# First split of x in the setup, a wait moved to its first use, and the gate weights' split moved from a batch's first slot to its third

## What is computed

```python
x = L0_conv(x)                      # 128x128 matrix over the channels, from a Ricker filter
t = to_tokens(x)                    # 16 batches, 1024 tokens, 128 channels
t = t + attn(ln(t))                 # linear attention, 8 heads of 16, elu+1 features, causal sums
t = t + ffn(ln(t))                  # per batch: weights W + sum_e g[b,e] * tv_W[e], g from the tokens' mean gate
x = from_tokens(t)

# in ffn
gh = relu(x @ gfc1_w.T + gfc1_b)
g  = (gh @ gfc2_w.T + gfc2_b).mean(over tokens)
W1m = W1 + einsum('be,efd->bfd', g, tv_W1)      # W2m likewise
```

## Time and profile before

| | |
|---|---|
| Median of three runs | 802.8 us (801.71 to 803.27) |
| Profiled execution | 801.26 us, span 799.0 us |
| Setup block | to about 15.9 us |
| Attention block | about 15.9 to 526 us |
| FFN block | from about 526 us |
| Busy over the span | PE 728.1, DVE 676.8, ACT 658.5, POOL 537.4 us |
| `scores_lo` (L805), costliest group on DVE | 175.8 us, 256 times 687 ns |

### The profile page before, as it was taken

The page is one execution under the profiler, slowest core; times in us unless marked ns, Lnnn a source line. Parts: engine busy times, 40 slices in busy tenths (PEclk is TensorE's granted clock), DMA queues, the critical chain, the costliest instruction groups (busy, mean ns, idle before and its releaser), DMA issues. The chain is left out here.

```text
span 799.0 us, 38795 instructions
## 1 busy us (share of the span) xinstructions
PE 728.1 (91%) x11936; PEld 538.6 (67%) x11936; DVE 676.8 (85%) x2605; ACT 658.5 (82%) x1864; POOL 537.4 (67%) x1167
## 2 busy tenths in 40 slices
PE   3869999999999999999999999768999996999993
PEld 2446667667667667667677677556777776677773
DVE  4668899999999999999999999636989875788984
ACT  3658899999999999999999999736888865788884
POOL 2768889999999999999999999610333331133332
PEclk9989999999999999999999999869999999999998
DMA  3475676556566566566565564410122221022222
GB/s 99 91 133 107 136 125 140 125 129 140 129 128 140 128 130 137 128 132 134 128 136 130 131 138 99 91 44 1 41 82 82 80 88 54 1 82 81 81 78 76
DMA packets 202346, 82.63 MB, mean 103 GB/s; under 512 B 176076, under 2 KB 189551, under 8 KB 202232
## 3 DMA queue, kind: packets, MB, share of 16 engines
q1 hardware_dynamic: 202296, 81.99, 45.3%
HBM read 22.69 MB, written 17.30 MB: 50 GB/s over the span
## 5 line engine op out<-in xcount | busy, mean ns | idle before, releaser
L805 DVE SCALAR_TENSOR_TENSOR scores_lo<-p_a,scores_hi 128x512 f16<-128x512 f32 x256 | 175.8, 687 | 5.6 <-ACT scores_hi L701 2.4
L701 ACT ACTIVATE scores_hi<-p_a 128x512 f16<-128x512 f32 x256 | 157.8, 620 | 23.7 <-PE p_a L570 18.9
L1312 POOL TENSOR_TENSOR ffn_rstd_shift<-ffn_rstd_shift,consts 128x4 f32<-128x4 f32 x32 | 36.8, 1149 | 130.8 <-DVE ffn_rstd_shift L1271 130.8
L876 POOL CAST qk_parts<-qk_f 128x256 f16<-128x256 f32 x256 | 101.9, 400 | 6.3 <-issue 4.2
L886 POOL TENSOR_TENSOR qk_parts<-qk_f,qk_parts 128x128 f16<-128x128 f32 x256 | 104.6, 431 | 0.9
L1095 PE MATMUL psb<-merged_W_of_batch,h_hi 128*128 128x128 f16 x512 | 94.2, 220 | 4.2 <-DVE h_lo L1249 3.1
L1249 DVE TENSOR_TENSOR h_lo<-h_f,h_hi 128x512 f16<-128x512 f32 x128 | 95.6, 786 | 1.2 <-ACT h_hi L1152 1.2
L1141 ACT ACTIVATE h_f<-psb,merged_b_of_batch 128x512 f32<-128x512 f32 x128 | 87.2, 711 | 11.3 <-PE psb L1076 11.2
L1097 PE MATMUL psb<-merged_W_of_batch,h_lo 128*128 128x128 f16 x512 | 93.8, 219 | 0.0
L1096 PE MATMUL psb<-merged_W_of_batch,h_hi 128*128 128x128 f16 x512 | 93.8, 219 | 0.0
L587 PE MATMUL p_o<-v_parts,scores_hi 128*128 128x17 f16 x1024 | 90.1, 171 | 1.8 <-issue 0.3
(11 more groups left out here) (192 smaller groups left out, 2883.5 us busy)
## 6 DMA issues: line engine op xcount, KB each, us to landing
x_f<-in_x SPq DMA_DIRECT2D x32, 256.0 KB, 3.2
t_rows<-t SPq DMA_DIRECT2D x64, 128.0 KB, 2.0
t_back<-t_rows SPq DMA_DIRECT2D x32, 256.0 KB, 2.7
out<-out_tile SPq DMA_DIRECT2D x32, 256.0 KB, 2.0
tv_share<-in_L_ffn_tv_W SPq DMA_DIRECT2D x32, 128.0 KB
qkT_parts<-qk_parts SPq DMA_TRANSPOSE x128, 3.1
zT_hi_lo<-z_parts SPq DMA_TRANSPOSE x128, 2.3
base_ffn_weights<-in_L_ffn_W SPq DMA_DIRECT2D x2, 256.0 KB, 4.5
```

The source lines that it names most:

```text
L701: nc.scalar.activation(ah[:, t % 2, cols], p_a[:, cols], ACT.Relu).then_inc(ahi_ready[eo], 1)
L805: nc.vector.scalar_tensor_tensor(al[:, t % 2, cols], p_a[:, cols], 0.0, ah[:, t % 2, cols], ALU.max, ALU.subtract).then_inc(alo_ready[eo], 1)
L876: nc.gpsimd.tensor_copy(dst, src.unsqueeze(2).broadcast_to([P, NH, 2, DH])).then_inc(done, 1)
```

## The change

Three edits. The split of the first two tiles of x (`x_hi` on ACT, `x_lo` on POOL) moves from the attention block's first slot to the end of what ACT and POOL do in the setup block; the two buffers are allocated earlier for it. PE's wait for `state_cleared` moves from the block's start to the first `state`. `tv_hi` and `tv_lo` run in s2 instead of s0 of each batch, at the same places in the orders.

```diff
+        xh_ready, xl_ready = sem("xh_ready"), sem("xl_ready")
...
+            xh = sb(early, "x_hi", [P, 2, HALF * P], F16)
+            xl = sb(early, "x_lo", [P, 2, HALF * P], F16)
...
                     for pair in range(TILES // 2):
                         nc.gpsimd.memset(yt[:, 2 * pair, 0:1], 0.0).then_inc(t1_stored[pair], 16)
+                    pool.wait_ge(xh_ready, 1)
+                    nc.gpsimd.tensor_tensor(xl[:, 0, 0:2 * P], xf[:, 0, 0:2 * P], xh[:, 0, 0:2 * P], ALU.subtract)\
+                        .then_inc(xl_ready, 1)
...
                     nc.scalar.activation(bwh[:, :, :], bw[:, :, :], ACT.Copy, scale=WS).then_inc(s_bhi, 1)
+                    act.wait_ge(x_loaded[0], 16)
+                    nc.scalar.activation(xh[:, 0, 0:2 * P], xf[:, 0, 0:2 * P], ACT.Copy).then_inc(xh_ready, 1)
...
                         if n == 0 if isinstance(n, int) else False:
                             pe.wait_ge(ones_set, 1)
+                            pe.wait_ge(state_cleared, 1)
...
                     pe.wait_ge(ones_set, 1)
-                    pe.wait_ge(state_cleared, 1)
...
                     def split_x(b, t):            # on ACT, and the same on POOL
-                        if t % 2:
+                        if t % 2 or isinstance(b, int) and TILES * b + t == 0:
                             return
...
                     def tv_hi(b, t):              # and the same in tv_lo on DVE
-                        if t:
+                        if t != 2:
                             return
```

More of the change, by code:

```diff
@@ L343, in build @@
         with early, ExitStack() as pa_:
-            xh = sb(pa_, "x_hi", [P, 2, HALF * P], F16)
-            xl = sb(pa_, "x_lo", [P, 2, HALF * P], F16)
             eq = sb(pa_, "exp_qk", [P, 4, 2 * C])
@@ L369, in build @@
             sbank = p_s[:, 0:NP * 2 * VW].rearrange("p (a w) -> p a w", w=2 * VW)
-            (xh_ready, xl_ready, conv_done, in_done, bn1, mv1, ve1, rstd1, vhi_ready, exp_ready, relu_ready, vlo_ready,
+            (conv_done, in_done, bn1, mv1, ve1, rstd1, vhi_ready, exp_ready, relu_ready, vlo_ready,
              qk_ready, qhi_ready, khi_ready, lo_ready, su_done, state_cleared, sh_ready, sp_ready,
@@ L375, in build @@
                 sem(s) for s in (
-                    "xh_ready xl_ready conv_done in_done bn1 mv1 ve1 rstd1 vhi_ready exp_ready relu_ready vlo_ready "
+                    "conv_done in_done bn1 mv1 ve1 rstd1 vhi_ready exp_ready relu_ready vlo_ready "
                     "qk_ready qhi_ready khi_ready lo_ready su_done state_cleared sh_ready sp_ready "
```

## The result

Median 796.7 us (794.4 to 800.0, 12 runs) against 802.0 us (799.5 to 804.9, 12 runs): a ratio of 0.9931, 95% interval 0.9913 to 0.9949, or 5.3 us less (the interval is 4.1 to 7.0). The forecast was 5.7 less. The profiled executions differ by 5.0 (spans 799.0 and 794.0).

The account below looks back on a forecast made before the run. The prediction took a ring of POOL's even slot, then PE and DVE in the odd slot, as the bound. Fill -2.25 and loop -3.5 gave -5.75: 797.1 us against 802.8, forecast 794.5 to 799.5, wider range 791.5 to 801.3.

Parts of the forecast that it names:

- Fill, -2.25: Attention stage's start: first statistics 3.15 us earlier, less 0.56 for held POOL and 0.35 in the setup; net -2.25 us.
- the hold on POOL's casts: Batch 0, third slot: `tv_lo` holds POOL's `q_hi` from 20.18 to 20.74, costing the fill 0.56 us.
- the new place in batch 1: Batch 1's moved split, at 49, lies in ACT's pause of 6.73 us until 56.47; nothing gained or lost.
- rival D: Pause after batch 0 ends by something that doesn't move, so the fill's gain is lost: 799.3 us; chance 0.10.
- Collision in the setup: Setup: POOL's `x_lo` and DVE's subtraction at 12.44 exclude each other; cost 0 to 0.67 us, +0.35 taken.
- Loop, -0.25 a batch: Batches 2 to 15: first slot gains 0.75, third slot costs 0.50; net -0.25 a batch, -3.5 us for fourteen.
- rivals A: Third slot takes the split nearly free, state work missing there: cost 0.15, about 792.1 us; chance 0.15.
- B: Third slot costs what the first did, only the fill's -2.25 remains: about 800.5 us; chance 0.19.
- C: Third slot: POOL's hold and DVE's delay follow each other, cost 1.20 a batch: about 806.9 us; chance 0.06.
- The ring: Attention loop: POOL's even slot, then PE and DVE in the odd one, is the bound; DVE and ACT alone have room.
- The sum: Whole kernel: -2.25 of fill and -3.5 of loop make -5.75 us, 797.1 against the median of 802.8.
- The FFN half is only shifted.: FFN block after attention: only starts earlier, with no gain or loss of its own.

Follow-up runs that it names:

- e1: The changed kernel with the share's split back in the first slot, leaving the first split and the moved wait; ratio 0.9996, 801.4 us.
- e2: The kernel before, with only the share's split moved to the third slot; ratio 0.9931, 796.4 us.
- e3: The changed kernel with the share's split in the third slot in batch 0 alone, the first slot in later batches; ratio 0.9956, 799.0 us.
- e5: The changed kernel with the share's split in the second slot of every batch; ratio 0.9937.
- e6: The changed kernel with the share's split in the fifth slot of every batch; ratio 0.9961.
- e10: The changed kernel plus unread PE matmuls behind the last seven gates and while PE waits for the first merge's gates; ratio 0.9926, 796.1 us.
- e4: The changed kernel with POOL's `x_lo` in the setup waiting for DVE's `base_ffn_lo`; ratio 0.9928, 795.4 us.
- e7: The changed kernel with both parts of the share split for only 2 of 256 columns in batches 2 to 15; executed once, 797.2 us.
- e8: The changed kernel with the share's high part made for only 2 of 256 columns in batches 2 to 15; executed once, 799.9 us.
- e9: The changed kernel with the share's low part made for only 2 of 256 columns in batches 2 to 15; executed once, 797.0 us.

## Why the prediction held, and where it did not

- **Fill, -2.25.** Measured -2.25 at the first state. The chain named was right: transfer, `tv_hi`, `tv_lo`, `stats1`. With the share back in s0 (e1) all of the gain is gone; with only the share moved (e2) the fill gains 1.56. The setup lost 0.50 for the 0.35 assumed, of which 0.34 is the copy's and 0.16 was there before POOL's `x_lo` began; the hold on POOL's casts cost 0.47 for 0.56. One reading was off without harm: the new place in batch 1, put at 49, does not lie in ACT's pause, which began at 56.47 - 6.73 = 49.74. It came at 46.49, the pause ran from 47.67 to 53.95, and the lead of 2.52 at its end sinks rival D.
- **Collision in the setup.** In the changed kernel's profile it came with another instruction than I named: not the subtraction at 12.44 with two inputs in SBUF, but the copy with a factor in front of it, 0.57 for 0.23, because the base weights and so ACT came half a microsecond earlier than in the profiled run before. The named collision came as well, in both of the orders that the prediction left open: POOL first in e3, e5 and e6 (1.57 to 1.68 for 1.22; the setup's last DVE instruction 0.36 to 0.49 later than before), DVE first in e10 (`x_lo` 1.71, the end 0.01 later). So what this edit costs in the setup is 0 to 0.5 us by chance of when the base weights arrive (ACT's cast of them starts at 10.47 to 11.06), and the 0.35 was a fair middle. The Trainium skill (SBUF — State Buffer, Who interferes with whom) counts casts and copies with a factor among what can take the shared pair; the 0.57 and e4's 0.53 agree.
- **Loop, -0.25 a batch.** Measured -0.33. Taking it out of s0 gave 0.88 in that pair (0.75 taken, up to 0.83 allowed), putting it into s2 cost 0.54 (0.50 taken). That the delays in s2 lie beside each other and don't add was right, and e7, e8 and e9 show it best: either one alone costs nearly what both do. The pair of 7.78 sinks rivals A (7.3) and B and C (8.0 and more), and e3 shows that the loop's slots are part of the gain.
- **Why s2 is cheaper than s0** is shown only in part. The fifth slot, with state work on all engines, costs 0.66, so missing state work is part of it. But ACT's 0.52 did not vanish in the room that it leaves, as I expected of e9.
- **The ring.** I took POOL's even slot and the other engines' odd slot for one closed ring; then the second slot should have cost 0.5 to 0.8. It cost 0.35. In e5 the pair of s0 and s1 grows, and part of it comes back in the next pair. How is only argued: what comes late in s1 meets s2, where PE has no state work. The ring is a fair account of the even slots and no full model of the loop.
- **The sum.** The term mis-sized is the loop: 14 x 0.33 = 4.6 instead of 3.5. With the fill's 2.25 the parts make 6.9, and 5.3 was measured, with 7.0 as the interval's end. So the nearness of 796.7 to 797.1 is in part luck: the parts gave more than forecast, and some 1.6 us of it doesn't show in the median. Where it stays is open. Batches 2 and 3 and the FFN block each differ by some 4 us from trace to trace, whatever the edit, and the twelve times of the changed kernel spread over 5.6 us.
- **"The FFN half is only shifted."** In the pair of profiled executions it was not: 2.5 of 7.5 us were lost at the two merges, where the half-clock stretches fell on different work. Against e4, the changed kernel with one more wait, the same comparison gives a lead of 6.36 at the last gate and 6.0 at the end. Over all traces the block's time follows no edit of this case. So the sentence is neither shown nor refuted within that scatter, and the prediction had no allowance for it.

## What to carry to other kernels

Ask of a stage's first slot what it waits for that could be asked for earlier or used later; here a piece of side work, placed early in each engine's order, held up the whole fill by its transfer. When a piece of work is moved in a balanced loop, price both places by carrying the rows on, and look for delays that lie beside each other: several engines' parts can cost little more than one of them. And compare the lead at the end of each stage, not only the spans: it can shrink in a stage that no line of the change touches. Before calling that a cost of the change, look at the same stage in every other trace; here it took 270.9 to 275.0 us with the same code.

## What the hardware showed unasked

- POOL and DVE stopped each other in both directions. On POOL `rsqrt2` took 1.00 for 0.55, a cast 0.87 for 0.40, `z_lo` 0.93 for 0.43 and `x_lo` 1.71 for 0.67 (e10); on DVE a copy with a factor took 0.57 or 0.73 (e1) for 0.23, a cast 0.53 for 0.43 and the base weights' subtraction 1.65 for 1.22 (e3). Which one is held depends on little: `x_lo` at 12.36 held the subtraction of 12.47, `x_lo` at 12.50 was held by the one of 12.45.
- PE about 75% busy at a granted clock of 0.50 from 513 to 525 us did not bring the full clock back (e10). It came after PE had gone over to the merge's matmuls without gaps.
- The same stretch of PE work ran at different clocks in different executions: the first five merged banks took 5.47 us in the kernel before, 5.89 in e4 and 6.91 in the changed kernel.
